# A two-layer attention and expert kernel: a tile-ordered row table by a 0/1 matrix, earlier weight splits, and low parts moved to VectorE

## The reference

```python
x = x + _L0_xattn_ref(_layernorm(x), ...)   # attention over 1024 context rows and the 512 rows themselves
x = x + _L0_ffn_ref(_layernorm(x), ...)     # 8 experts, 2 per token, inner width 256
x = x + _L1_xattn_ref(_layernorm(x), ...)   # attention over the context alone
x = x + _L1_ffn_ref(_layernorm(x), ...)     # 32 experts, 8 per token, inner width 192
# one expert step, for each token t and each of its chosen experts e:
h = silu(xt @ w_gate[e]) * (xt @ w_up[e])
out[t] += weight[t, e] * (h @ w_down[e])
```

## Time and profile before

| what | value |
|---|---|
| median of three runs | 1075.88 us (1073.94 to 1077.32) |
| the profiled execution, its own time | 1072.7 us |
| its span, first to last instruction | 1071.0 us |
| TensorE busy | 793.9 us, 74% |
| VectorE, ScalarE, GpSimd busy | 516.0, 524.1, 498.8 us |
| mean granted TensorE clock | 0.912 |

### The profile page before, as it was taken

The page is one execution under the profiler, slowest core; times in us unless marked ns, Lnnn a source line. Parts: engine busy times, 40 slices in busy tenths (PEclk is TensorE's granted clock), DMA queues, the critical chain, the costliest instruction groups (busy, mean ns, idle before and its releaser), DMA issues.

```text
span 1071.0 us, 20194 instructions
## 1 busy us (share of the span) xinstructions
PE 793.9 (74%) x5086; PEld 427.6 (40%) x5087; DVE 516.0 (48%) x1523; ACT 524.1 (49%) x782; POOL 498.8 (47%) x413
## 2 busy tenths in 40 slices
PE   4998999997289983769872177777787787767770
PEld 3444455543144441335341143444444444434440
DVE  5653545565444623657763243444544535453432
ACT  5532334544357741345542155566656565655550
POOL 4870001001357755004665545666766566666560
PEclk9999999999599995979886598999999999999995
DMA  8553010000358868311110358878898887879668
GB/s 286 176 171 118 11 40 21 31 30 31 111 150 212 219 108 232 126 40 41 32 42 23 100 129 212 209 162 211 210 239 198 197 199 182 175 197 243 150 110 256
DMA packets 108390, 150.72 MB, mean 141 GB/s; under 512 B 18336, under 2 KB 59552, under 8 KB 108352
## 3 DMA queue, kind: packets, MB, share of 16 engines
q1 hardware_dynamic: 80000, 93.49, 26.8%
q0 software_dynamic: 25760, 56.56, 26.8%
q10 hardware_dynamic: 2592, 0.19, 0.2%
HBM read 107.34 MB, written 42.86 MB: 140 GB/s over the span
## 4 chain that ended last, share of the span: by engine, by line
PE 37%; DMA 16%; issue 14%; DVE 10%; DVEq 9%; ACT 5%; SPq 4%; POOL 3%; ACTq 2%; another core or an unknown queue 1%; POOLq 0%
PE pst L187 31%; DMA big<-in_L_ffn_w_down_dram 7%; DMA x_rows<-mid,small 4%; DVEq L1154 4%; DMA mid<-moe_normalised_rows,small 3%; DVEq L1148 3%; POOL moe_tokens_of_experts L988 2%; PE pst L1258 2%; PE pst L489 2%; DMA big<-x_rows 1%; PE pst L947 1%; DVE big L1140 1%; ACT mid L1294 1%; SPq L1086 1%
## 5 line engine op out<-in xcount | busy, mean ns | idle before, releaser
L187 PE MATMUL pst<-big,mid 128*128 (+1 forms) x1392 | 280.8, 354 | 22.3 <-DVE mid L1369 12.9
L1452 POOL DMA_INDIRECT x_rows<-mid,small x100 | 160.3, 1603 | 126.9 <-ACT mid L1313 68.0
L988 POOL DMA_INDIRECT moe_tokens_of_experts<-token_no,small x80 | 82.7, 1033 | 288.1 <-DVE small L1041 267.6
L187 PEld LDWEIGHTS pst<-big,mid 128*128 128x128 f16 x1392 | 135.9, 100 | 132.8 <-issue 38.9
L1442 POOL DMA_INDIRECT mid<-moe_normalised_rows,small x106 | 113.8, 1074 | 98.2 <-DVE small L1359 41.3
L1258 PE MATMUL pst<-big,mid 128*128 x520 | 131.9, 387 | 1.5 <-ACT mid L1305 0.9
L1294 ACT ACTIVATE mid<-pst 128x1024 f16<-128x1024 f16 x102 | 103.7, 1017 | 57.1 <-PE pst L1230 49.1
L1230 PE MATMUL pst<-id,mid 128*128 128x128 f16 x816 | 65.9, 227 | 64.0 <-DMA mid<-moe_normalised_rows,small 56.0
L1369 DVE SCALAR_TENSOR_TENSOR mid<-pst,small,mid 128x192 f32<-128x192 f32 (+1 forms) x100 | 42.6, 426 | 118.8 <-ACT mid L1300 102.3
L187 PE MATMUL pst<-ctxN,mid 128*128 128x512 f16 x384 | 93.5, 404 | 3.2 <-ACT mid L613 3.2
L1230 PEld LDWEIGHTS pst<-id,mid 128*128 128x128 f16 x816 | 55.3, 102 | 97.3 <-issue 41.8
(11 more groups left out here) (199 smaller groups left out, 1165.6 us busy)
## 6 DMA issues: line engine op xcount, KB each, us to landing
big<-in_L_ffn_w_gate_dram SPq DMA_DIRECT2D x32, 384.0 KB
big<-in_L_ffn_w_up_dram SPq DMA_DIRECT2D x32, 384.0 KB
big<-in_L_ffn_wi_dram SPq DMA_DIRECT2D x16, 512.0 KB
big<-in_L_ffn_w_down_dram SPq DMA_DIRECT2D x32, 256.0 KB
big<-in_L_ffn_w_down_dram SPq DMA_DIRECT2D x64, 128.0 KB
moe_normalised_rows<-xn SPq DMA_DIRECT2D x18, 256.0 KB, 2.0
mid<-in_ctx_dram SPq DMA_DIRECT2D x16, 256.0 KB, 3.9
big<-in_ctx_turned_dram SPq DMA_DIRECT2D x16, 256.0 KB, 4.5
```

The lines of the kernel that those rows point to most:

```text
L187: last = nc.tensor.matmul(dst, stationary(a, c), moving(b, c), start=(k == 0), stop=(k == 3 * len(parts) - 1))
L988: nc.gpsimd.indirect_dma_start(out=self.tab_d[:, :], out_offset=bass.IndirectOffsetOnAxis(ap=self.addr[j % 2][:, k:k + 1], axis=0), in_=to ...
L1452: nc.gpsimd.indirect_dma_start(out=acc_d[p][:, :], out_offset=bass.IndirectOffsetOnAxis(ap=self.si[p], axis=0), in_=self.y[p], in_offset=N ...
```

## The change

1. **The table in tile order.** After the table has come back, it is cast to float16, transposed on TensorE, and multiplied with a 0/1 matrix `sel` that picks for each tile its column. The result, `rows`, holds the token numbers of tile t in column t. So VectorE no longer reads columns from `ctab`; `row_numbers` forms its address from the loop counter. `ftab` is gone too.
2. **h split at once.** `h_high` and `h_low` of tile t follow `make_h`(t). `rows_out`(t-2) is now first in the tile's turn on VectorE.
3. **Weights three experts ahead.** A new row `stab` is `etab` plus 3. When a tile's expert is finished, ScalarE and VectorE split the expert four further on, into the buffer that became free.
4. **Low parts on VectorE.** In the loop `split_lo` makes both low parts; GpSimd has only gathers and scatters there.
5. **Second expert stage: splits during attention.** Experts 0 to 3 are split in `attn1` (`split_early_hi` on ScalarE, `split_early_lo` on GpSimd, whole), and SP loads experts 2 to 5 inside `norm_sp`.
6. **Routing order.** `logits` stands in the middle of `values`; `choose` comes at the end of a tile's turn, one tile earlier; the last tiles' order is changed; constants are made at the start of the kernel; the spare rows are written after the first list.

The core of the diff:

```diff
+                dst, n = bank(7 if self.first else 6 + i % 2), 4 * self.nc_
+                half = n // 2
+                three(pe, dst, range(half), lambda h, k: pT[:, h, k, :], val, final=False)
+                between()
+                three(pe, dst, range(half, n), lambda h, k: pT[:, h, k, :], val, first=False).then_inc(self.pv_full, 1)
...
+                    if not self.first and 1 <= i <= 4:
+                        self.next.split_early_hi(act, i - 1)
...
+                    if not self.late and j in (1, 2, 4, 5):
+                        e = {1: 2, 2: 3, 4: 4, 5: 5}[j]
+                        self.load_next(sp, e, e % 2)
...
+            def split_early_lo(self, pool, e):
+                pool.wait_ge(self.w_hi, 2 * e + 2)
+                nc.gpsimd.tensor_tensor(self.gu[:, e, 1, :, :], self.gur[:, e % 2, :, :], self.gu[:, e, 0, :, :], ALU.subtract).then_inc(self.wgu_lo, 1)
+                nc.gpsimd.tensor_tensor(self.d[:, e, 1, :, :], self.dr[:, e % 2, :, :], self.d[:, e, 0, :, :], ALU.subtract).then_inc(self.wd_lo, 1)
+
+            def split_lo(self, dve, e):
+                r, s = e % 2, e % 4
+                dve.wait_ge(self.w_hi, 2 * e + 1)
+                nc.vector.tensor_tensor(self.gu[:, s, 1, :, :], self.gur[:, r, :, :], self.gu[:, s, 0, :, :], ALU.subtract).then_inc(self.wgu_lo, 1)
+                dve.wait_ge(self.w_hi, 2 * e + 2)
+                nc.vector.tensor_tensor(self.d[:, s, 1, :, :], self.dr[:, r, :, :], self.d[:, s, 0, :, :], ALU.subtract).then_inc(self.wd_lo, 1)
...
+                pe.wait_ge(self.tab_s, 3)
+                nc.tensor.matmul(bank(4)[:, 320:320 + NE], ones16[0:1, :], self.crow, start=True, stop=True).then_inc(self.route_pe, 1)
+                pe.wait_ge(self.rows_s, 1)
+                for q in range(self.NQ):
+                    last = nc.tensor.transpose(bank16(3)[0:self.CQ, q * P:(q + 1) * P], self.tab16[:, q * self.CQ:(q + 1) * self.CQ], id16[:])
+                last.then_inc(self.route_pe, 1)
+                pe.wait_ge(self.rows_s, 2)
+                for q in range(self.NQ):
+                    nc.tensor.matmul(bank(5)[:, 0:NE], self.tabT[0:self.CQ, q, :], self.sel[0:self.CQ, q, :], start=(q == 0), stop=False)
+                nc.tensor.matmul(bank(5)[:, 0:NE], spare16[:], self.over, start=False, stop=True).then_inc(self.route_pe, 1)
...
             def dve_pair(self, dve, it, first):
 
-                e = self.experts(dve, it, 0, 3)
-                c = self.columns(dve, it, -2, 7)
+                e = self.experts(dve, it, 1, 2)
+                x = None if first else self.splits(dve, it)
                 for p in range(2):
                     t = 2 * it + p
-                    self.rows_in_turn(dve, it + 1 + p, t + 3, 1 - p, c[5 + p])
-                    self.weights_in_turn(dve, it + 1 + p, t + 1, 1 - p, e[1 + p])
-                    if not (first and p == 0):
-                        self.h_high(dve, t - 1, 1 - p)
-                        self.h_low(dve, t - 1, 1 - p)
-                    with dve.If(e[p + 1] > e[p]):
-                        self.split_d_lo(dve, e[p + 1])
+                    if not first:
+                        self.rows_out(dve, it - 1, t - 2, p)
+                    self.rows_in_turn(dve, it + 1 + p, t + 3, 1 - p)
+                    self.weights_in_turn(dve, it + 1 + p, t + 1, 1 - p, e[p])
                     self.make_h(dve, t, p)
-                    if not first:
-                        self.rows_out(dve, it - 1, t - 2, p, c[p])
+                    self.h_high(dve, t, p)
+                    self.h_low(dve, t, p)
+                    if first:
+                        if self.late:
+                            self.split_d_lo(dve, 2 + p)
+                    else:
+                        with dve.If(x[p + 1] > x[p]):
+                            self.split_lo(dve, x[p + 1])
...
+            exp1.split_early_lo(pool, 0)
+            exp1.split_early_lo(pool, 1)
             for j in range(NT):
                 exp1.list_tokens(pool, j)
-            pool.wait_ge(attn1.x_s, NT)
+                if j < 2:
+                    exp1.split_early_lo(pool, 2 + j)
+                if j == 0:
+                    exp1.spare_rows(pool)
             exp1.pool(pool)
```

More of the change, by code:

```diff
@@ L180, in program, with three @@
         PASSES = [(0, 0), (0, 1), (1, 0)]
-        def three(pe, dst, parts, stationary, moving):
+        def three(pe, dst, parts, stationary, moving, first=True, final=True):
             k, last = 0, None
@@ L186, in three @@
                 for a, b in PASSES:
-                    last = nc.tensor.matmul(dst, stationary(a, c), moving(b, c), start=(k == 0),
-                                            stop=(k == 3 * len(parts) - 1))
+                    last = nc.tensor.matmul(dst, stationary(a, c), moving(b, c), start=(first and k == 0),
+                                            stop=(final and k == 3 * len(parts) - 1))
                     k += 1
@@ L724, in dve @@
                         norm2.normalise(dve, 3)
-                    if self.first and i >= 3:
-                        self.next.choose(dve, i - 3)
                     if i >= 1:
@@ L735, in dve @@
                         self.next.place(dve, i - 3)
-                    if not self.first and i >= 2:
-                        self.next.choose(dve, i - 2)
                     self.move_second(dve, i)
@@ L753, in dve @@
                         self.next.norm_low(dve, i - 1)
+                    if i >= (2 if self.first else 1):
+                        self.next.choose(dve, i - (2 if self.first else 1))
                 if self.first:
-                    self.next.choose(dve, NT - 3)
                     self.readout_low(dve, NT - 1)
@@ L1151, in experts, with splits @@
                 return values
-            def columns(self, eng, it, first, n):
+            def splits(self, eng, it):
                 _, values = nc.values_load_multi_w_load_instructions(
-                    self.ctab[0:1, bass.ds(2 * it + first + 2, n)], engines=[eng.engine], min_val=0,
-                    max_val=NT * self.E, skip_runtime_bounds_check_because="the columns are kept within the table")
-                return values
-            def first_tile(self, eng, e):
-                return eng.value_load(self.ftab[0:1, bass.ds(e, 1)], min_val=0, max_val=NT * self.K + self.E + self.CR)
+                    self.stab[0:1, bass.ds(2 * it, 3)], engines=[eng.engine], min_val=0,
+                    max_val=self.E - 1, skip_runtime_bounds_check_because="the experts of the table are below E")
+                return values
             def pairs(self, eng):
@@ L1315, in act_pair @@
             def act_pair(self, act, it, first):
-                e = self.experts(act, it, 2, 3)
+                e = None if first else self.splits(act, it)
                 for p in range(2):
@@ L1417, in dve @@
-                dve.wait_ge(self.tab_in, 32)
-                for t in range(3):
-                    self.rows_in_turn(dve, t // 2 or None, t, t % 2, c[t])
-                self.weights_in_turn(dve, 1, 0, 0, e[0])
-                with dve.If(e[1] > 0):
+                self.rows_in_turn(dve, None, 0, 0)
+                self.rows_in_turn(dve, None, 1, 1)
+                if self.late:
                     self.split_d_lo(dve, 1)
+                self.weights_in_turn(dve, 1, 0, 0, 0)
+                self.rows_in_turn(dve, 1, 2, 0)
@@ L1460, in pool_pair, with spare_rows, pool @@
                     self.gather(pool, t + 3, 1 - p)
-                    with pool.If(e[p + 1] > e[p]):
-                        self.split_gu_lo(pool, e[p + 1])
-                    if not first:
+                    if first:
+                        if self.late:
+                            self.split_gu_lo(pool, 2 + p)
+                    else:
                         self.scatter(pool, it - 1, t - 2, p)
-            def pool(self, pool):
-                self.pool_constants(pool)
-                self.split_gu_lo(pool, 0)
+            def spare_rows(self, pool):
+                pool.wait_ge(self.before, 1)
                 for q in range(2):
                     pool.dma_start(acc_d[q][NT * P:(NT + 1) * P, :], x_sb[:, 0, :]).then_inc(self.scat[q], 16)
+            def pool(self, pool):
+                if self.late:
+                    self.split_gu_lo(pool, 0)
                 np_ = self.pairs(pool)
-                _, e1 = self.experts(pool, 0, 0, 2)
-                with pool.If(e1 > 0):
+                self.gather(pool, 0, 0)
+                self.gather(pool, 1, 1)
+                if self.late:
                     self.split_gu_lo(pool, 1)
-                for t in range(3):
-                    self.gather(pool, t, t % 2)
+                self.gather(pool, 2, 0)
                 self.pool_pair(pool, 0, True)
```

274 lines of the change are left out of this document (144 added, 130 removed).

## The result

The changed kernel takes 1129.74 us (median of 4 runs, 1124.96 to 1132.16) against 1074.91 us before: a ratio of 1.0491 with a 95% interval of 1.0453 to 1.0529. Timed again, beside other kernels, it came to 1.051 [1.0439, 1.0581]. Forecast were 1025 us and, with a chance of 0.92, a gain; it is a loss of 55 us.

What follows compares the result with a forecast made beforehand. It took the scatter-to-gather circle to pace the second loop at 4.85 us a tile. Gains of 38.7 + 5.3 + 1 + 5.5 = 50.5 us from 1072.7 gave 1022.2, plus 3.2 for the median: 1025 us, range 996 to 1060.

Steps and rivals of the forecast that it cites:

- the second loop's term: Second expert stage's tile loop: 5.34 falls to 4.85 us a tile over 79 steps, 38.7 us gained, ends 74 and 0.
- The new order's price: Both loops: scatter wait now precedes the gather's index, a four-tile circle of 4.4 to 5.35 us a tile, middle 4.85.
- Low parts on VectorE: Second loop: 2.96 us an expert on VectorE, about 4.2 us busy a tile, above TensorE's 3.66; no gain booked.
- 5 and 21 times: Second loop: single late transfers seen before the change were few, so the middle between calm and full DMA was taken.
- circle of scatter, index and gather: Rival, second loop: late scatters and slower gathers make 5.6 us a tile, total 1085 us; slower had chance 0.05.
- The 44.5 us go: Second loop: splitting h right after make_h hides it behind matmuls, removing TensorE's 44.5 us of waits for h's low part.
- My circle through make_h: Theory from the follow-ups, not the prediction: make_h, index copies, gather and back set the loops' pace, about 15 to 16 us per three tiles.
- The first loop: First expert stage: same edits bring it to 4.85 us a tile, gaining 5.3 us, ends 0 and 10.
- attn1 and the second routing: Between the loops: lists end 4 to 5 us earlier and a shorter chain follows; 5.5 us gained, ends 10 and −5.
- in that idle time or ahead of it: Second attention layer: GpSimd's four early splits, 22 us, fit its some 26 us of idle time between or before lists.
- ScalarE's wait for raw weights: Second loop: three experts in stock remove 26.4 us of waits; at most 10 us counted as gain, at least nothing.
- DMA was not the bound: Rival, second loop: DMA engines limit it to 4.8 or 5.14 us a tile; with returned waits, chance 0.20.

Runs made afterwards that it cites:

- the fast kernel: Changed kernel without early splits, VectorE's turn in the order of before, low parts one tile behind the high parts: 0.9828 of the kernel before.
- the low parts out of the way: Changed kernel with low parts one tile after the high parts and placed ahead of make_h: 1.0205 of the kernel before.
- the single experiment: Only rows_out moved ahead of rows_in_turn, on the fast kernel: 1.0501 of the kernel before.
- the run with a lag of one tile: Changed kernel with VectorE making an expert's low parts one tile after ScalarE's high parts, in both loops: 1.0264 of the kernel before.
- The run with the stand-ins: The fast kernel plus GpSimd subtracts of the early splits' size that feed nothing, and two clears, in the second attention layer: 0.9997 of the kernel before.

## Why the prediction was wrong

**The step that failed: the second loop's term, 79 × (5.34 − 4.85) = 38.7 us.** It took the circle from scatter to gather ("The new order's price", 4.4 to 5.35 us a tile, the middle of it) for the only thing that sets the pace, and put VectorE under it by its busy time ("Low parts on VectorE": "That is about 4.2, under today's 5.34"). Measured were 5.62 us a tile, a loss of 21.9 us.

**What it priced at nothing: low parts and high parts in one tile.** The 2.96 us an expert were right (1.76 + 1.22). But it didn't ask what the instruction waits for, nor what is queued behind it. Undoing the coupling on the changed kernel is worth 0.19 us a tile of the second loop (5.62 to 5.43), placing the low part ahead of make_h 0.18 more (5.25). That kernel still has the scatter's index first and h split at once, and its loop is already faster than before. The step from there to scatter index last and no early splits brings 0.15 (5.10). On the fast kernel the coupling alone costs 0.12 of the time. The prices depend on each other: with the coupling in place, moving the index to the end cost 0.046; without it, having it there gains.

**The circle.** The few late scatters ("5 and 21 times") were no evidence, since the old place of `rows_out` was what kept them few: moved to the front, the wait rose from 6.6 to 82.7 us in the change, 117.0 with the low parts out of the way, and 183.8 us in the single experiment. That experiment costs 0.88 us a tile (4.99 to 5.87), but by way of the split of h, which the change doesn't have behind the wait. No run shows the circle through the gather as the pace of a loop; that its middle, 4.85, was too low is shown, for the kernel with the low parts out of the way ran at 5.25, and where the remaining 0.4 come from stays open. One term was also read wrong: 6.43 us run from the start of one gather, at 605.48, to a landing that the chain counts from the start of the next, at 606.81; from its own start a gather takes 5.10 us there, and the circle comes to 4.1 and 5.0 us a tile. The rival "circle of scatter, index and gather", with a chance of 0.05, gave 5.6 us a tile for 5.62 measured. That is luck: 0.37 of it hang on the low parts, and its total of 1085 missed the losses in the first loop and in attn1.

**"h split at once" was to take away 44.5 us of waiting ("The 44.5 us go"), and is worth nothing**: +0.044 alone on the kernel before, ±0 on the fast kernel, −0.066 where a long wait began the turn. TensorE's wait for h did fall; what ended next was a gather. Why it costs so much on the kernel before isn't settled. What differs there is, among other things, GpSimd's subtract between gather and scatter, ten register reads, and low parts made in another tile. My circle through make_h would explain it; on the fast kernel h at once and later reads speak against that circle, on the kernel before it was never tried alone.

**The first loop**: +17.9 us where −5.3 was booked. I wrote that ScalarE waits "in the first pair, where TensorE was idle anyway". The profile shows 10.6 and 8.5 us for the third and fourth step instead of 4.6 and 5.0. ScalarE waits for no weights there; it casts at 300.76 and 305.15 us, and behind its casts VectorE and GpSimd make their shares of the low part side by side, so that for each of these experts one operation of VectorE takes 3.1 us for 1.2:

```profile
309.14 2.27 POOL L1150 TENSOR_TENSOR big<-big 128x1024 f16<-128x1024 f32 x1
```

```profile
309.35 3.14 DVE L1159 TENSOR_TENSOR big<-big 128x1024 f16<-128x1024 f32 x1
```

Behind them stands the copy for the next gather. Moving these splits to later tiles, and off GpSimd, took 0.013 (14 us) off the whole time. The coupling of low and high parts costs in this loop too: the run with a lag of one tile took 5.51 us a tile for 6.08, 11 us in all.

**attn1 and the second routing**: +16.7 us where −5.5 was booked. Split costs of 5.5 us on GpSimd (5.2 measured) and the 7.5 us from the last list to the first gather (644.44 − 636.82 = 7.6) were right. But the first list began at 520.20, not near 498, and GpSimd then still waited 20.4 us for places:

```profile
520.20 1.02 POOL L1011 DMA_INDIRECT moe_tokens_of_experts<-token_no,small  x1 [0.16 <-issue]
...
635.86 0.96 POOL L1011 DMA_INDIRECT moe_tokens_of_experts<-token_no,small  x1 [0.30 <-issue]
644.44 1.01 POOL L1482 DMA_INDIRECT mid<-moe_normalised_rows,small  x1 [7.62 <-DVE small L1391]
```

The wrong sentence is that GpSimd's 22 us of splits lie "in that idle time or ahead of it": the idle time covers GpSimd's own work, but not what that work does to VectorE, on which the layer's chain lies. The prediction had the rule in hand for the loop and not for the layer. The Trainium skill ("SBUF — State Buffer", Who interferes with whom) says that a VectorE instruction with two SBUF inputs and a GpSimd instruction that reads SBUF exclude each other for the whole instruction; the trace agrees (128x32 in 3.11 us beside a subtract of 3.10). The run with the stand-ins shows that GpSimd's work alone makes the 16 us, and the operations held add up to them: 16.8 us in the changed kernel, 15.8 in that run. Tables in tile order and the new places of `choose` gave nothing that can be seen: 221.6 us between the loops without early splits, 221.3 with the old code in the same group (one profile each).

**What was right**: ScalarE's wait for raw weights is gone (26.4 us before, none in the second loop's list); low parts on VectorE don't hurt in themselves (0.983 with them); DMA was not the bound (a share of 0.74, and 0.84 on the fast kernel).

## What to carry to other kernels

Price an instruction on an in-order queue by three things: how long it runs, what it waits for, and what stands behind it; a copy of 0.15 us in the wrong place cost 6.7%. Rare waits at a place say nothing about that place once the instruction is moved; and removing TensorE's most frequent wait gains only if the next thing in line was ready. A work split over two engines (high part, low part) wants a tile between its halves, and idle time of GpSimd is no free room while VectorE works on the critical chain.

## What the runs showed of the hardware

- VectorE's 128x32 operations with two SBUF inputs, 0.19 to 0.25 us alone, took up to 3.98 us beside GpSimd subtracts of 2.1 to 3.1 us; four pairs of them and two clears lengthened a stretch of 225 us by 16.
- TensorE's mean granted clock goes with the waits: 0.95 in the second loop of the kernel before, 0.88 in the changed one, 0.94 in that of 0.983. In the changed kernel a gate_up behind a wait of 4.20 us for rows took 3.70 us (at 804.98 us), the next one 2.11.
- One chip of five spent some 19 us less between the loops than the others on the same code (219 for 238, and 203 for 222 without early splits). Its profiles show no wait between the loops whose releaser is unknown; the others do, up to 13.9 us at one place (`choose`'s copy, in the run with the stand-ins, and 13.1 with h at once on the fast kernel, where GpSimd subtracts nothing there). What they wait for is not known. The early splits cost 16 us on either kind of chip.
